# The last projection of layer 1 in PSUM banks of its own, and the final normalisation spread over VectorE, ScalarE and GpSimd

## The chip, the cores and the metric

One core of one Trainium2 chip runs the kernel. The metric is the device time of one execution in microseconds. A core has TensorE (matrix products, abbreviated PE in the profile, PEld for its weight loads), VectorE (DVE), ScalarE (ACT), GpSimd (POOL) and SyncE (SP), each with an instruction queue of its own; they wait for each other by semaphores. SBUF is the on-chip memory of 128 partitions, PSUM holds what TensorE puts out, in eight banks of 512 floats per partition.

## The reference, cut to what matters

A sequence of 2048 tokens with 256 features goes through two layers. Each has cross attention to 1601 context rows (16 heads), added through a gate, and a mixture of experts, added through another gate. Layer 1, which the change touches, is:

```python
out = jnp.einsum('bhnm,bmhd->bnhd', attn, v).reshape(B, N, IMAGE_DIM)
h = jax.nn.relu(out @ W1 + b1)              # 256 -> 512
return h @ W2 + b2                          # 512 -> 256: the attention's result
...
logits = jnp.einsum('bsd,de->bse', x, Wg) + bg
topk_vals, topk_idx = jax.lax.top_k(logits, TOP_K)      # 2 of 8 experts
topk_w = jax.nn.softmax(topk_vals, axis=-1)
h = jax.nn.relu(jnp.einsum('bsd,edf->bsef', x, W1) + b1)
eo = jnp.einsum('bsef,efd->bsed', h, W2) + b2
sel = jnp.take_along_axis(eo, topk_idx[..., None], axis=2)
mixed = jnp.sum(sel * topk_w[..., None], axis=2)
y = mixed + x
mu = jnp.mean(y, axis=-1, keepdims=True)
var = jnp.mean(jnp.square(y - mu), axis=-1, keepdims=True)
return gamma * (y - mu) * jax.lax.rsqrt(var + LN_EPS) + beta
...
x = x + jnp.tanh(g_ffn[1]) * _L1_ffn_ref(_layernorm(x, axis=-1), ...)
```

## The kernel before

The 2048 tokens lie as 16 tiles of 128 tokens, a token to a partition; four tiles make a block (four blocks). `x` is the running state, `xn` (a part of `xt`) its normalised copy. The program is a sequence of stages (`nc.Block()`), each ended by a barrier of all engines; within one, each engine's work is written out in order by hand, with semaphores between them. Nothing reorders it.

In the attention stage of a layer, TensorE makes scores and weighted sums for block after block. The projection of block b - 1 is woven into the scores of block b by `tail`: for layer 1 four calls of `hidden` (the 512 hidden features in four pieces of 128, each a product into PSUM bank 7, which VectorE reads through the relu into `hidT`) and then `output` for two pairs of tiles, also into bank 7, which VectorE reads into `y_tmp` and adds to `x`. Each piece waits for `s_read7`, that is until VectorE has read the one before. For the last block there are no more scores to weave into, so `for w in range(NC + 1): tail(NB, w)` runs the pieces one after the other. VectorE's part is `tail(NB, NB - 1)` at lines 1213 to 1240: after the updates it normalises the block (`norm_rows`), then come the transposes, the router's logits, the counts and slots of the routing, and GpSimd's 32 scatters of the tokens into the experts' lists.

The expert stage works through 39 tiles of 128 rows. For tile i, SyncE loads the rows, TensorE turns them (line 1542), VectorE copies them (1622), TensorE makes the first product (1555), VectorE adds the bias (1652), ScalarE takes the relu (1610), TensorE makes the second product (1567), VectorE adds its bias (1674), and GpSimd scatters the rows to `y_tok` with an indirect DMA (1738), which waits until the previous scatter has landed. In VectorE's order, `place` (lines 1634 and 1637: two instructions on one column that compute the row to which the result goes) stands between `hidden` and `finish`.

After the last scatter SyncE reads the results back, per block two reads of 512 KB (line 1515) into `got[0]` and `got[1]`, the second and first choice of each token. VectorE alone then does, for each block: `xn` plus weight times `got[0]` (1715), plus weight times `got[1]` (1720), statistics of the rows (421, 424), the reciprocal root by three Newton steps on four columns (426 to 436), the subtraction and scaling (439), times gamma (1727), plus beta (1728, gate folded into both by lines 1702 and 1703), and the addition to `x` (1729); SyncE writes the block out (1527).

## Time and profile before

| quantity | value |
|---|---|
| median of three runs | 1559.49 us (1559.07 to 1561.18) |
| profiled execution, its own time | 1561.43 us |
| its span, first to last instruction | 1559.7 us |
| TensorE busy | 1329.1 us (85%) |
| ScalarE busy | 958.1 us (61%) |
| VectorE busy | 576.2 us (37%) |
| GpSimd busy | 149.4 us (10%) |
| mean granted TensorE clock | 0.926 of full speed |

The profile is of one execution. Busy times add up what an engine's instructions took; a share averages over stages with different limits, so a change is read from the stage in which it lies. Times in the rows below are microseconds from the span's start.

### The profile page before, as it was taken

What the parts mean: (1) busy time and instruction counts of PE and PEld (TensorE: products, weight loads), DVE (VectorE), ACT (ScalarE), POOL (GpSimd) and SP (SyncE); (2) the same over time, 40 slices, a digit from 0 to 9 for tenths busy, and PEclk for the clock granted to TensorE, in tenths of its full rate; (3) what the DMA queues carried; (4) which work ended last, traced back from release to release, by engine and by line L of the source; (5) the groups of instructions that cost most, each with busy time, mean ns of one, the idle gap of its engine ahead of it and who ended that gap; (6) DMA issues with size and microseconds to landing.
All of it is one profiled execution on the core that took longest, in us unless ns stands there. A gap on an engine that the chain in (4) does not pass through costs nothing. (4 is left out here: it accounts for less than half of the span.)

```text
span 1559.7 us, 31895 instructions
## 1 busy us (share of the span) xinstructions
PE 1329.1 (85%) x13108; PEld 695.6 (45%) x13108; DVE 576.2 (37%) x1403; ACT 958.1 (61%) x1114; POOL 149.4 (10%) x157
## 2 busy tenths in 40 slices
PE   6899999999999988997479999999999750599920
PEld 4433333333335548996233343333343230499920
DVE  7412242331523433444522224224233232244458
ACT  3599999999993332332279969959969600244400
POOL 2000000000002341222000000000000005222210
PEclk9899999999999998999689999999999875799965
DMA  7680101010107141114186100100111132122241
GB/s 211 154 192 20 25 19 26 19 26 19 33 21 252 38 158 58 49 49 108 58 201 167 26 15 19 27 14 19 27 44 49 55 122 78 62 76 69 74 140 40
DMA packets 88875, 111.48 MB, mean 71 GB/s; under 512 B 10746, under 2 KB 75006, under 8 KB 87960
## 3 DMA queue, kind: packets, MB, share of 16 engines
q1 hardware_dynamic: 83448, 94.93, 22.5%
q0 software_dynamic: 5280, 14.47, 2.5%
q8 instruction: 107, 1.75, 0.5%
q14 instruction: 40, 0.33, 0.1%
HBM read 68.06 MB, written 36.81 MB: 67 GB/s over the span
## 5 line engine op out<-in xcount | busy, mean ns | idle before, releaser
L1119 ACT ACTIVATE arena<-ps 128x1024 f32<-128x1024 f32 x556 | 557.0, 1241 | 57.3 <-PE ps L917 57.3
L917 PE MATMUL ps<-arena 99*32 99x512 bf16 x6656 | 464.4, 384 | 13.6 <-PEq L767 9.6
L917 PEld LDWEIGHTS ps<-arena 99*32 99x32 bf16 x6656 | 150.1, 95 | 405.9 <-issue 166.9
L1119 ACT ACTIVATE wqkv<-ps 128x1024 f32<-128x1024 f32 x276 | 297.4, 1243 | 22.7 <-PE ps L917 22.7
L933 PE MATMUL ps<-arena 128*32 128x512 f32 x2224 | 289.3, 594 | 0.8 <-ACT arena L1119 0.8
L1201 DVE COPY work<-ps 128x512 f32<-128x512 f32 x32 | 22.1, 692 | 402.6 <-PE ps L933 402.6
L1555 PEld LDWEIGHTS ps<-work,arena 128*128 128x128 f32 x1184 | 144.6, 195 | 6.5 <-DVE work L1622 3.5
L1555 PE MATMUL ps<-work,arena 128*128 128x128 f32 x1184 | 145.7, 279 | 2.1 <-DVE work L1622 2.1
L933 PE MATMUL ps<-wqkv,arena 128*32 128x512 f32 x1104 | 143.2, 593 | 0.0
L1567 PE MATMUL ps<-arena,work 128*128 x496 | 117.2, 380 | 0.0
L1205 DVE RECIPROCAL work<-work 128x512 f32<-128x512 f32 x32 | 107.3, 3353 | 1.1
L1593 ACT ACTIVATE arena<-arena 128x1024 f32 x62 | 65.3, 1057 | 65.5 <-PEq L897 56.8
L1480 POOL DMA_INDIRECT list_x<-xt,slot x48 | 46.3, 964 | 579.4 <-DVE slot L1341 565.2
L933 PEld LDWEIGHTS ps<-arena 128*32 128x32 f32 x2224 | 68.2, 111 | 59.3 <-ACT arena L1119 2.7
L1567 PEld LDWEIGHTS ps<-arena,work 128*128 128x128 f32 x496 | 89.4, 190 | 10.1 <-issue 0.5
L1738 POOL DMA_INDIRECT y_tok<-work,dest x62 | 62.6, 1010 | 256.0 <-DVE work L1672 130.0
L1542 PE MATMUL ps<-ident,work 128*128 128x128 f32 x124 | 24.5, 281 | 62.5 <-DMA work<-list_x 62.5
L1622 DVE COPY work<-ps 128x256 f32<-128x256 f32 x62 | 26.3, 425 | 137.3 <-PE ps L1542 137.3
L1610 ACT ACTIVATE work<-work 128x512 f32<-128x512 f32 x39 | 24.6, 631 | 82.2 <-DVE work L1652 82.2
L1604 ACT ACTIVATE work<-ps 128x512 f32<-128x512 f32 x23 | 13.7, 597 | 89.3 <-PE ps L1555 89.3
L1468 POOL TENSOR_TENSOR arena<-arena 128x512 f32<-128x512 f32 x12 | 17.5, 1458 | 490.3 <-ACT arena L1139 490.3
L1226 DVE TENSOR_TENSOR work<-ps,b 128x512 f32<-128x512 f32 x16 | 11.1, 692 | 111.6 <-PE ps L958 111.6
(185 smaller groups left out, 1125.3 us busy)
## 6 DMA issues: line engine op xcount, KB each, us to landing
arena<-in_ew SPq DMA_DIRECT2D x16, 512.0 KB, 5.3
work<-list_x SPq DMA_DIRECT2D x62, 129.0 KB, 2.1
arena<-q_img SPq DMA_DIRECT2D x32, 192.0 KB
arena<-y_tok SPq DMA_DIRECT2D x12, 512.0 KB, 7.4
list_x<-zero SPq DMA_DIRECT2D x1, 5160.0 KB, 36.2
arena<-k_img SPq DMA_DIRECT2D x8, 624.0 KB, 12.4
q_img<-work SPq DMA_DIRECT2D x18, 256.0 KB, 2.5
k_img<-work SPq DMA_DIRECT2D x21, 208.0 KB, 2.4
```

The source lines that it names most:

```text
L917: last = nc.tensor.matmul(ps[i * VW:(i + 1) * VW, buf + j, :], k2[0:ROWS + SHIFT, h, at:at + VW], q2[0:ROWS + SHIFT, h, :], start=True, st ...
L933: last = nc.tensor.matmul(ps[j * VW:(j + 1) * VW, 6 + g % 2, :], v_aug[:, c, HG * g + j, :], probs[(b * STEPS + 2 * w + j // 2) % RING][:, ...
L1119: nc.scalar.activation(probs[(b * STEPS + u) % RING], ps[:, buf:buf + 2, :], ACT.Exp, scale=SCALE).then_inc(s_exp, 1)
L1205: nc.vector.reciprocal(sums, sums).then_inc(s_inv, 1)
L1480: nc.gpsimd.indirect_dma_start(out=list_x[l], out_offset=bass.IndirectOffsetOnAxis(ap=slot[:, i:i + 1], axis=0), in_=xt[:, i % NT, :], in_ ...
L1542: last = nc.tensor.transpose(ps[:, i % 2, k * P:(k + 1) * P], rows_in[i % 2][:, k * P:(k + 1) * P], ident[:, :])
L1555: last = nc.tensor.matmul(ps[:, 2 + 2 * (i % 2) + n, f * P:(f + 1) * P], w_now[i % 2][n][:, k, f * P:(f + 1) * P], rowsT[i % 2][:, k, :], ...
L1567: last = nc.tensor.matmul(ps[:, 6 + i % 2, 0:D], hT[i % 2][:, k, :], w_down[:, bass.ds(e, 1), k, :].rearrange("p a n -> p (a n)"), start=( ...
L1593: nc.scalar.activation(w_now[i % 2][0].rearrange("p k n -> p (k n)"), w_gate[l][:, bass.ds(e, 1), :, :].rearrange("p a k n -> p (a k n)"), ...
L1610: nc.scalar.activation(hT[i % 2], act_g[i % 2], ACT.Relu).then_inc(s_h, 1)
L1622: nc.vector.tensor_copy(rowsT[i % 2], ps[:, i % 2, 0:D].rearrange("p (k n) -> p k n", n=P)).then_inc(s_tc, 1)
L1738: nc.gpsimd.indirect_dma_start(out=y_tok[l], out_offset=bass.IndirectOffsetOnAxis(ap=dest[:, i % 4:i % 4 + 1], axis=0), in_=rows_out[i % 2 ...
```

## The change

It has three parts. First, the last block's projection of layer 1 is no longer made by `tail` but by a new `last_projection`: the four hidden pieces go to PSUM banks 0 to 3 without a wait between them, and the four output tiles to banks 4 to 7, with the loop over the hidden pieces outside, each waiting for its piece's relu. VectorE reads these banks (`own`).

Second, in the expert stage of layer 1, the scaling of gamma and beta by the gate goes to the start of VectorE's queue, and GpSimd adds beta to `x`, block by block, ahead of its first scatter.

Third, the final normalisation: ScalarE multiplies `got[0]` by its weight, GpSimd adds `xn`, VectorE adds `got[1]` times its weight and makes the statistics. The root is made once for eight tiles (`norm_root`, twice instead of four times), and gives a scale and a shift per row (`norm_scales`). ScalarE applies them tile by tile, GpSimd multiplies by gamma for two tiles at a time, and VectorE adds the product to `x` for two tiles at a time, all of it after the scales of both halves. SyncE's reads and writes stay.

```diff
@@ -100,6 +100,7 @@
         xt = sb("xt", [P, NT, DX])
         xn = xt[:, :, 0:D]
         zero = sb("zero", [P, DX])
+        scales = sb("scales", [P, 2, NT])
         dest_f = sb("dest_f", [P, 4])
         dest = sb("dest", [P, 4], U32)
         ctxT = sb("ctxT", [CH + 1, 2, MP])
@@ -414,12 +415,8 @@
             nc.gpsimd.iota(iota_tile[:, :], pattern=[[P, 48]], base=0, channel_multiplier=0,
                            allow_small_or_imprecise_dtypes=True)
-        def norm_rows(step, src, dst, n=TB):
-            for t in range(n):
-                last = nc.vector.bn_stats(stats[:, t, :], src(t))
-            step(last)
+        def norm_root(step, n):
             for t in range(n):
                 last = nc.vector.bn_aggr(mv[:, t, :], stats[:, t, :])
             step(last)
@@ -435,10 +432,29 @@
                 step(nc.vector.tensor_tensor(newton[:, 0:n], newton[:, 0:n], var_h[:, 0:n], ALU.mult))
                 step(nc.vector.scalar_tensor_tensor(out=rstd[:, 0:n], in0=newton[:, 0:n], scalar=1.5,
                                                     in1=rstd[:, 0:n], op0=ALU.add, op1=ALU.mult))
+        def norm_rows(step, src, dst, n=TB):
+            for t in range(n):
+                last = nc.vector.bn_stats(stats[:, t, :], src(t))
+            step(last)
+            norm_root(step, n)
             for t in range(n):
                 last = nc.vector.tensor_scalar(dst(t), src(t), mv[:, t, 0:1], rstd[:, t:t + 1], ALU.subtract,
                                                ALU.mult)
             return last
+        def norm_scales(step, src, n, scale, shift):
+            for t in range(n):
+                last = nc.vector.bn_stats(stats[:, t, :], src(t))
+            step(last)
+            norm_root(step, n)
+            nc.vector.tensor_copy(scale, rstd[:, 0:n])
+            return nc.vector.scalar_tensor_tensor(out=shift, in0=mv[:, 0:n, 0], scalar=-1.0, in1=rstd[:, 0:n],
+                                                  op0=ALU.mult, op1=ALU.mult)
         def layer(L):
             l = L.n
@@ -1064,9 +1080,28 @@
                         pe.wait_ge(s_ks, KD * (n + 1))
                         norm_sums(ps[:, 3, n * 4 * H:(n + 1) * 4 * H], squares1[n % 2], KC).then_inc(s_kn, 1)
+                    def last_projection():
+                        for i in range(2):
+                            pe.wait_ge(s_oc[i], NB * 16 * HG * NG // 2)
+                        pe.wait_ge(s_u, NB * NG)
+                        for f in range(4):
+                            for k in range(KD):
+                                last = nc.tensor.matmul(ps[:, f, :], w1[:, k, f * P:(f + 1) * P], oT[:, k, :],
+                                                        start=(k == 0), stop=(k == KD - 1))
+                            last.then_inc(s_full7, 1)
+                        for f in range(4):
+                            pe.wait_ge(s_read7, use(NB, f))
+                            for t in range(TB):
+                                last = nc.tensor.matmul(ps[:, 4 + t, 0:D],
+                                                        hidT[:, f, t * P:(t + 1) * P], w2[:, f, :],
+                                                        start=(f == 0), stop=(f == 3))
+                                if f == 3 and t % 2 == 1:
+                                    last.then_inc(s_full7, 1)
                     if l == 1:
-                        for w in range(NC + 1):
-                            tail(NB, w)
+                        last_projection()
                         last_turn()
                         last_logits()
                         counts()
@@ -1215,15 +1250,17 @@
                         group(now, NG - 1)
                         k = 0
+                        own = L.mlp and b == NB
                         if L.mlp:
                             for f in range(4):
                                 dve.wait_ge(s_full7, use(b, k))
-                                nc.vector.tensor_scalar(hidT[:, f, :], ps[:, 7, :], b1[:, f:f + 1], 0.0,
+                                nc.vector.tensor_scalar(hidT[:, f, :], ps[:, f if own else 7, :], b1[:, f:f + 1], 0.0,
                                                         ALU.add, ALU.max).then_inc(s_read7, 1)
                                 k += 1
                         for pair in range(2):
                             dve.wait_ge(s_full7, use(b, k))
                             nc.vector.tensor_tensor(y_tmp.rearrange("p (t d) -> p t d", d=D),
+                                                    ps[:, 4 + 2 * pair:6 + 2 * pair, 0:D] if own else
                                                     ps[:, 7, :].rearrange("p (t d) -> p t d", d=D), b2[:, :, :],
                                                     ALU.add).then_inc(s_read7, 1)
                             dve.wait_ge(s_read7, use(b, k))
@@ -1490,6 +1527,9 @@
+            s_gb, s_xb = sem(f"norm_params_scaled{l}"), sem(f"x_with_beta{l}")
+            s_w0, s_w1, s_sc = sem(f"first_weighed{l}"), sem(f"first_added{l}"), sem(f"norm_scales{l}")
+            s_nr, s_gm = sem(f"rows_normed{l}"), sem(f"rows_scaled_gamma{l}")
@@ -1614,6 +1654,18 @@
                         for c in range(NC):
                             act.wait_ge(s_v, c + 1)
                             copy_v(c, c % 4).then_inc(s_va, 1)
+                    else:
+                        for b in range(NB):
+                            act.wait_ge(s_back[b], 16 * L.top)
+                            for t in range(b * TB, (b + 1) * TB):
+                                last = nc.scalar.activation(got[0][:, t, :], got[0][:, t, :], ACT.Identity,
+                                                            scale=wts[:, 2, t:t + 1])
+                            last.then_inc(s_w0, 1)
+                        for t in range(NT):
+                            act.wait_ge(s_sc, t // (2 * TB) + 1)
+                            nc.scalar.activation(got[0][:, t, :], got[0][:, t, :], ACT.Identity,
+                                                 bias=scales[:, 1, t:t + 1], scale=scales[:, 0, t:t + 1]
+                                                 ).then_inc(s_nr, 1)
                 @block.vector
                 def _(dve):
@@ -1675,6 +1727,11 @@
                                                     eb2[:, bass.ds(e, 1), :].rearrange("p a n -> p (a n)"), ALU.add
                                                     ).then_inc(s_y, 1)
+                    tg = tgate[:, 2 + l:3 + l]
+                    chain = Chain(dve, f"back_chain{l}")
+                    if l == 1:
+                        nc.vector.tensor_scalar(gamma, gamma, tg, None, ALU.mult)
+                        nc.vector.tensor_scalar(beta, beta, tg, None, ALU.mult).then_inc(s_gb, 1)
                     copy_rows(0)
                     if l == 0:
                         copy_up(0)
@@ -1696,40 +1753,43 @@
                             copy_up(i + 2)
                     finish(NTL - 1)
-                    tg = tgate[:, 2 + l:3 + l]
-                    chain = Chain(dve, f"back_chain{l}")
-                    if l == 1:
-                        nc.vector.tensor_scalar(gamma, gamma, tg, None, ALU.mult)
-                        chain(nc.vector.tensor_scalar(beta, beta, tg, None, ALU.mult))
-                    for b in range(NB):
-                        ts = slice(b * TB, (b + 1) * TB)
-                        dve.wait_ge(s_back[b], 16 * L.top)
-                        if l == 0:
+                    if l == 0:
+                        for b in range(NB):
+                            ts = slice(b * TB, (b + 1) * TB)
+                            dve.wait_ge(s_back[b], 16)
                             chain(nc.vector.scalar_tensor_tensor(
                                 out=x[:, ts, :].rearrange("p t d -> p (t d)"),
                                 in0=got[0][:, ts, :].rearrange("p t d -> p (t d)"), scalar=tg,
                                 in1=x[:, ts, :].rearrange("p t d -> p (t d)"), op0=ALU.mult, op1=ALU.add))
                             chain(norm_rows(chain, lambda t: x[:, b * TB + t, :], lambda t: xn[:, b * TB + t, :]))
-                            continue
-                        for t in range(b * TB, (b + 1) * TB):
-                            last = nc.vector.scalar_tensor_tensor(out=xn[:, t, :], in0=got[0][:, t, :],
-                                                                  scalar=wts[:, 2, t:t + 1], in1=xn[:, t, :],
-                                                                  op0=ALU.mult, op1=ALU.add)
-                        chain(last)
-                        for t in range(b * TB, (b + 1) * TB):
-                            last = nc.vector.scalar_tensor_tensor(out=got[0][:, t, :], in0=got[1][:, t, :],
-                                                                  scalar=wts[:, 1, t:t + 1], in1=xn[:, t, :],
-                                                                  op0=ALU.mult, op1=ALU.add)
-                        chain(last)
-                        chain(norm_rows(chain, lambda t: got[0][:, b * TB + t, :], lambda t: got[0][:, b * TB + t, :]))
-                        gb = gamma.unsqueeze(1).broadcast_to([P, TB, D])
-                        bb = beta.unsqueeze(1).broadcast_to([P, TB, D])
-                        chain(nc.vector.tensor_tensor(got[0][:, ts, :], got[0][:, ts, :], gb, ALU.mult))
-                        chain(nc.vector.tensor_tensor(x[:, ts, :], x[:, ts, :], bb, ALU.add))
-                        nc.vector.tensor_tensor(x[:, ts, :], x[:, ts, :], got[0][:, ts, :], ALU.add).then_inc(s_xf, 1)
+                    else:
+                        n = 2 * TB
+                        for i in range(2):
+                            for b in range(2 * i, 2 * i + 2):
+                                dve.wait_ge(s_w1, b + 1)
+                                for t in range(b * TB, (b + 1) * TB):
+                                    last = nc.vector.scalar_tensor_tensor(out=got[0][:, t, :], in0=got[1][:, t, :],
+                                                                          scalar=wts[:, 1, t:t + 1],
+                                                                          in1=got[0][:, t, :], op0=ALU.mult,
+                                                                          op1=ALU.add)
+                            chain(last)
+                            norm_scales(chain, lambda t: got[0][:, i * n + t, :], n, scales[:, 0, i * n:(i + 1) * n],
+                                        scales[:, 1, i * n:(i + 1) * n]).then_inc(s_sc, 1)
+                        for t in range(0, NT, 2):
+                            dve.wait_ge(s_gm, t // 2 + 1)
+                            last = nc.vector.tensor_tensor(x[:, t:t + 2, :], x[:, t:t + 2, :], got[0][:, t:t + 2, :],
+                                                           ALU.add)
+                            if t % TB == TB - 2:
+                                last.then_inc(s_xf, 1)
                 @block.gpsimd
                 def _(pool):
+                    if l == 1:
+                        pool.wait_ge(s_gb, 1)
+                        for b in range(NB):
+                            nc.gpsimd.tensor_tensor(x[:, b * TB:(b + 1) * TB, :], x[:, b * TB:(b + 1) * TB, :],
+                                                    beta.unsqueeze(1).broadcast_to([P, TB, D]), ALU.add
+                                                    ).then_inc(s_xb, 1)
                     for i in range(NTL):
                         pool.wait_ge(s_de, i + 1)
                         pool.wait_ge(s_y, i + 1)
@@ -1741,6 +1801,17 @@
                     if l == 0:
                         ones_row(pool, 2)
                         pad_v(Chain(pool, "v_pad_chain1"))
+                    else:
+                        for b in range(NB):
+                            ts = slice(b * TB, (b + 1) * TB)
+                            pool.wait_ge(s_w0, b + 1)
+                            nc.gpsimd.tensor_tensor(got[0][:, ts, :], got[0][:, ts, :], xn[:, ts, :], ALU.add
+                                                    ).then_inc(s_w1, 1)
+                        for t in range(0, NT, 2):
+                            pool.wait_ge(s_nr, t + 2)
+                            nc.gpsimd.tensor_tensor(got[0][:, t:t + 2, :], got[0][:, t:t + 2, :],
+                                                    gamma.unsqueeze(1).broadcast_to([P, 2, D]), ALU.mult
+                                                    ).then_inc(s_gm, 1)
         for L in layers:
```

## Rows read from the trace of the kernel before

**Rows 1.** Chain of work that ended last: start us, duration us, what.
```profile
1495.93 2.41 DMA y_tok<-work,dest
...
1498.83 4.99 DMA arena<-y_tok
...
1508.77 0.39 DVE mv L424 x4
...
1511.44 0.17 DVE root_bits L436
...
1553.94 1.23 DVE x L1729
```

**Rows 2.** Timeline, GpSimd: start us, us, engine, line, operation, [idle before <- released by].
```profile
1354.75 0.96 POOL L1738 DMA_INDIRECT y_tok<-work,dest  x1 [19.05 <-DVE work L1674]
```

**Rows 3.** Timeline, last projection of layer 1.
```profile
1244.35 3.75 PE L945 MATMUL ps<-work,w 128*128 128x512 f32 x4 [9.49 <-issue]
...
1253.57 1.98 PE L945 MATMUL ps<-work,w 128*128 128x512 f32 x4 [0.85 <-DVE work L1221]
...
1259.32 3.69 PE L958 MATMUL ps<-w,work 128*128 128x256 f32 x16 [0.94 <-DVE work L1221]
...
1269.20 1.41 DVE L421 BATCH_NORM_STATS2 stats<-x 128x6 f32<-128x256 f32 x4
```

**Rows 4.** Stretches: us; busy PE, PEld, DVE, ACT, POOL; PE clock; DMA.
```profile
1252.00:1253.00 1.00, 0.73 (x1) 0.00 (x0) 0.23 (x1) 0.00 (x0) 0.00 (x0) 0.67 1.10 364
...
1348.00:1349.00 1.00, 0.48 (x3) 0.14 (x2) 0.42 (x1) 0.00 (x0) 0.00 (x0) 0.88 0.00 0
```

**Rows 5.** Timeline, start of layer 1's expert stage.
```profile
1340.81 3.98 SPq L1504 DMA_DIRECT2D work<-list_x  x3
...
1349.77 0.20 DVE L1634 TENSOR_SCALAR dest_f<-work,tilef 128x1 f32<-128x1 f32 x1
```

**Rows 6.** Timeline, two GpSimd additions in layer 0's shared expert.
```profile
497.23 0.72 POOL L1473 TENSOR_TENSOR x<-x,arena 128x256 f32<-128x256 f32 x1 [0.84 <-ACT arena L1148]
...
499.93 1.27 POOL L1468 TENSOR_TENSOR arena<-arena 128x512 f32<-128x512 f32 x1 [0.25 <-ACT arena L1139]
```

**Rows 7.** Timeline, GpSimd and VectorE beside each other.
```profile
525.23 4.29 DVE L1306 TENSOR_SCALAR xt<-xt,wts 128x256 f32<-128x256 f32 x16
...
527.18 3.46 POOL L1468 TENSOR_TENSOR arena<-arena 128x512 f32<-128x512 f32 x1 [2.68 <-ACT arena L1139]
...
535.44 0.29 DVE L1337 TENSOR_TENSOR work<-work,padc 128x128 f32<-128x128 f32 x1
535.60 1.27 POOL L1468 TENSOR_TENSOR arena<-arena 128x512 f32<-128x512 f32 x1 [3.62 <-ACT arena L1139]
535.76 1.25 DVE L1339 TENSOR_TENSOR work<-work,oh 128x128 f32<-128x128 f32 x1
```

**Rows 8.** Groups by shape: busy us, mean ns | idle before (L1211: 1234 to 1275.5).
```profile
L1715 DVE SCALAR_TENSOR_TENSOR xt<-arena,wts,xt 128x256 f32<-128x256 f32 x16 | 6.7, 478 | 10.1 <-DMA arena<-y_tok 10.1
L421 DVE BATCH_NORM_STATS2 stats<-arena 128x6 f32<-128x256 f32 x16 | 5.6, 414 | 0.1
...
L1211 DVE TENSOR_TENSOR work<-work 128x512 f32<-128x512 f32 x1 | 0.7, 693 | 0.1
...
L1593 ACT ACTIVATE arena<-arena 128x1024 f32 x62 | 65.3, 1057 | 65.5 <-PEq L897 56.8 <-issue 6.6
L1610 ACT ACTIVATE work<-work 128x512 f32<-128x512 f32 x39 | 24.6, 631 | 82.2 <-DVE work L1652 82.2
```

**Rows 9.** Reads of expert rows: timeline row, then the issue's KB and us to landing.
```profile
1499.92 0.51 SPq L1515 DMA_DIRECT2D arena<-y_tok  x1
arena<-y_tok SPq DMA_DIRECT2D x1, 512.0 KB, 8.2
...
1504.88 1.83 SPq L1515 DMA_DIRECT2D arena<-y_tok  x1
arena<-y_tok SPq DMA_DIRECT2D x1, 512.0 KB, 9.1
```

## The prediction, made before the changed kernel was run

> **What bounds the kernel now.** I read the chain of work that ended last first, from its end backwards. It ends in VectorE: from the landing of the first expert rows at 1503.8 us to the last addition at 1555.2 us nothing but VectorE works [rows 1]. Before that lies one read of 5 us, and before that a chain of scatters: the first of layer 1's 39 starts at 1354.75 us, released by the first tile's result [rows 2], the last at 1495.93 us, to land at 1498.34 [rows 1]. So one scatter and its wait take (1498.34 - 1354.75)/39 = 3.68 us. In the waits of that stretch nearly every scatter is released by the landing of the one before; the chain view hands over to TensorE at 1405 us, where it names the scatter's destination column, but that column is for a tile still to come. TensorE needs about as much per tile, so I take the whole stretch as a stiff piece: it starts when the first scatter starts and its length stays. The third place is the last projection of layer 1's attention, between 1244.35 and 1269.20 us [rows 3]: there TensorE and VectorE take turns on one PSUM bank, and all that follows (routing, lists, experts) waits. The change touches these three places and nothing else on the path.
>
> **Part 1, last projection in its own banks.** Before, one hidden piece is made, VectorE reads it, the next one is made. After, the sixteen TensorE instructions of the four hidden pieces are issued without a wait, and then the 32 of the output, ordered by piece, so that they need piece 3 only for their last eight. At the high clock four 512-column instructions took 1.98 us and sixteen 256-column ones 3.69 [rows 3]: with p for 512 columns and e for the pipeline's end, 4p + e = 1.98 and 8p + e = 3.69, so p = 0.43 and e = 0.27. At the low clock p is 0.86 (there four took 3.75). What decides is when the granted clock goes from 1.2 to 2.4 GHz. Before, it did in the slice 1252 to 1253 (mean 0.67, so at 1252.7), 8.3 us after TensorE's start at 1244.35 with one pause of 0.8 us. At the start of layer 1's experts it rose at 1348.25 (mean 0.88 of the slice 1348 to 1349) [rows 4], 4 to 5.5 us after the first dense work. With a rise at 1252.7, ten hidden instructions run low and six high: 8.6 + 2.6 = 11.2 us, to 1255.5; with a rise at 1248.5, five low and eleven high: 4.3 + 4.7 = 9.0, to 1253.3. The output adds 32 x 0.215 + 0.25 = 7.1 us: end at 1262.6 or 1260.4. VectorE's four relus (one pass over 512 columns each, about 0.7 us [rows 8]) hide under the later hidden pieces and the first 24 output instructions. At the end, though, both pairs are ready nearly together: the first 0.86 us before the second, and each needs an addition and an update, about 1.5 us together. So statistics start about 2.2 us after TensorE's end, where before they started one such pair of passes, 1.5 us, after it: 1264.8 or 1262.6 instead of 1269.2, a gain of 4.4 to 6.6 us. I take 5.5, between the two observed rises, since TensorE is now busier than in the first case. The pause until the transposes stays about 8 us, so the low clock there stays too.
>
> **Part 2, start of layer 1's expert stage.** The two scalings of gamma and beta go ahead of VectorE's first tile. The stage's first transfer is issued at 1340.81 [rows 5]; VectorE then waits for rows that TensorE can only turn after that transfer has landed, so they cost nothing. New on GpSimd's queue, ahead of all 39 scatters, are four additions of beta on 128x1024. GpSimd's 128x512 addition takes 1.27 us and its 128x256 one 0.72 [rows 6], so 1024 columns by the same slope take 1.27 + 2 x 0.55 = 2.37 us: 9.5 us for four, from about 1341.8 (the transfer's issue, and two scalings of 0.4) to 1351.3. The first scatter came at 1354.75, so about 3 us of cover are left. The other path is the shared access of the two engines to SBUF. When VectorE worked from 525.23 to 529.52, a GpSimd addition begun at 527.18 took 3.46 us instead of 1.27, that is until VectorE's stream ended; the other way, VectorE's 128x128 product with both inputs in SBUF took 1.25 us beside a GpSimd addition, against 0.29 for the same shape alone [rows 7]. Each waits out the other. In the expert loop the two small instructions of each tile that compute the destination (lines 1634, 1637) have all operands in SBUF, and they stand between the rows' copy and the result's copy in VectorE's order. The first tile's pair stands in VectorE's long wait for TensorE's second tile, where two waits of at most 2.37 us nearly fit. The second tile's pair, at 1349.8 [rows 5], meets the last addition: it ends at about 1352.0 instead of 1350.2, of which VectorE's later slack leaves about 0.5 us for the first result. Bounds: 0, and 2.5 us (one whole addition). I take 0.5, all of which shifts the scatters.
>
> **Part 3, the final normalisation.** I lay it out in the old time scale, with GpSimd and VectorE excluding each other wherever VectorE has all operands in SBUF. Prices: VectorE's weighted sum of 256 columns 6.7/16 = 0.42, its statistics 5.6/16 = 0.35 (one input, not excluded), an addition of 512 columns 0.69 [rows 8], four aggregations 0.39 and the root after them, to 1511.61, 2.4 us whatever the number of rows [rows 1]; GpSimd 2.37 and 1.27 as above; ScalarE 0.63 us for 512 and 1.06 for 1024 columns [rows 8], so 0.42 for 256, some 0.33 of it in a stream. Block 0 is in at 1503.8 [rows 1], block 1 at 1499.92 + 8.2 = 1508.1, block 3 at 1504.88 + 9.1 = 1514.0 [rows 9], block 2 between, about 1511.
> - ScalarE weighs block 0 to 1505.3, GpSimd adds to 1507.7. Block 1: ScalarE 1509.5, GpSimd 1511.9. VectorE's sums of block 0 lie between; those of block 1 run 1511.9 to 1513.6 and hold GpSimd's third addition back to 1513.6 to 1516.0; the fourth ends 1518.4.
> - VectorE: eight statistics and eight aggregations to 1517.3, the root held until 1518.4, then 2.4 + 0.35 us: first scales at 1521.2.
> - VectorE's eight sums of blocks 2 and 3 to 1524.6, which hold GpSimd's gamma products; these run 1524.6 to 1529.9 (four, 1.27 each). Statistics to 1528.2, the root mostly behind those products: second scales at 1532.5.
> - VectorE's four first additions to 1535.2; then four products and four additions in turns, 4 x (1.27 + 0.69) = 7.9 us, to 1543.1.
> The end was 1555.2, so the part gains 12 us. GpSimd gets 4 x 2.37 + 8 x 1.27 = 19.6 us of work, and VectorE keeps 16 x 0.42 + 5.6 + 1.6 + 2 x 2.75 + 8 x 0.69 = 24.9. The last transfer is as large as before, and its 4.5 us to the end stay.
>
> The rows show this exclusion for a stream of TENSOR_SCALARs and for one TENSOR_TENSOR [rows 7], not for a wide SCALAR_TENSOR_TENSOR. If the latter did not hold GpSimd, the third addition would end at 1514.9, the first four products at 1526.5, and the last addition at about 1541, a gain of 14. The Trainium skill, page "SBUF — State Buffer", section "Who interferes with whom", says that any VectorE instruction with two SBUF inputs contends with a GpSimd instruction that reads SBUF and that the later one blocks fully; by it the gain is 12. No row here tests that shape.
>
> **Sum.** On the profiled execution: 1561.43 - 5.5 + 0.5 - 12.0 = 1544.4 us. Its span is 1559.7, with 1.7 outside; the median of the runs, 1559.49, lies 1.9 below it, so the same sum on the median is 1542.5.
>
> **Rivals.**
> - A, the exclusion is weaker than laid out (long additions do not hold each other). Then the same schedule without holds gives first scales at 1520.1, second at 1529.9, the last addition at 1536.4: gain 18.8, in all 5.5 + 18.8 - 0.2, that is 1535.4. Against it stand both pairs of [rows 7]; for it, that they show few shapes.
> - B, exclusion worse: every stretch of GpSimd and VectorE in the tail is serial. 24.9 (VectorE) + 19.6 (GpSimd) + 2.1 (ScalarE) = 46.6 us from 1503.8: end at 1550.4, gain 4.8. With 4.4 from the projection and 2.5 lost at the start: 1559.5 - 6.7 = 1552.8. Against it: statistics and transfers do overlap.
> - C, slower than before: GpSimd's price for 128x1024 is not on the line through 256 and 512. Place: the four additions ahead of the scatters, then the tail. With a factor s on all GpSimd work the start costs 9.5s - 13.0 + 0.5 (13.0 from 1341.8 to the first scatter), the tail 19.6(s - 1) - 12; with -5.5 the sum is zero at s = 1.7, that is 4.0 us for 128x1024; at s = 2 it is +8.6, 1568.1. The two measured sizes lie on a plain line with a small constant, so I give it little.
> - D, the projection brings nothing, since the clock stays low through it (16 x 0.86 + 32 x 0.43 + 0.5 = 28.0 us of TensorE, and 1.5 for VectorE: statistics at 1273.9, 4.7 later than before): -12 + 0.5 + 4.7, 1552.7. Against it, the rise came in both examples within 8.3 us.
>
> **How the numbers follow.** Forecast 0.65, A 0.17, B 0.10, C 0.04, D 0.04. The range leaves out most of B, C and D: low 1535.0, from A; high 1549.0, from the forecast with its bad ends (-4.4 + 2.5 - 9, where 9 is midway between the 12 laid out and the 5 of B, a bit above). Under 0.2%, 3 us, this kernel's change can't be told from none. Faster by more is all but C and the worst of B and D: 0.95; same 0.02; slower 0.03.
>
> **What would show it.** Part 1: one stretch of TensorE without pauses from the first hidden piece to the last output, statistics 18.3 to 20.5 us after its start, against 24.9. Part 2: first scatter 13.9 to 16.5 us after the stage's first transfer, against 13.9; GpSimd's additions at 2.4 us, lines 1634 and 1637 stretched to about 2 us for one or two tiles. Part 3: GpSimd's products stretched beside VectorE's weighted sums, the small root instructions stretched beside products, and some 39 us from block 0's landing to the last addition, against 51.4. The prediction is wrong if GpSimd's 128x1024 takes over 3 us, if the scatter chain gets longer in itself, or if additions and products run side by side.

## The result, and the profile after

The changed kernel takes 1543.19 us (median of four, three of them 1541.6 to 1544.5) beside 1559.28 for the kernel before (1557.18 to 1561.18): a ratio of 0.9893, 95% interval 0.9876 to 0.9910, or 16.7 us less. Forecast were 1542.5 us and a range of 1535.0 to 1549.0.

Three executions took much longer than the others of their kernel (3394.7 us here, and beside the experiments 3008.46 of the kernel before and 1701.61 of e2) and enter no ratio, and as the profile that came with these runs is of the first of them, in which TensorE's products took over twice their usual time (the bf16 ones 0.79 us each for 0.38), "after" below (e1) is a further execution of the same kernel, beside which the kernel before was run on the same chip.

> The changed kernel once more, to read its stages at the usual TensorE clock. Theory (sum of parts -5.5, +0.5, -12): about 1542.5 us; projection stretch from TensorE's first hidden instruction to the statistics 18.3 to 20.5 us; first scatter about 14.4 us after the expert stage's first transfer; block 0's landing to last addition 41 us. Rival (the whole gain comes from the tail, the projection gains nothing because of the clock): the first stretch stays at 24 to 29 us and the tail is under 35 us.

Measured: 1549.74 us (1547.28 to 1551.87) on a chip where the kernel before takes 1566.34; ratio 0.9894 [0.9876, 0.9912]. Its page, span and two of the engines:

```profile
span 1547.6 us, 31882 instructions
PE 1326.8 (86%) x13108; PEld 695.4 (45%) x13108; DVE 563.7 (36%) x1345; ACT 973.0 (63%) x1146; POOL 179.8 (12%) x173
```

GpSimd has 30 us more of work, ScalarE 15, VectorE 13 less, though VectorE's busy time holds waits for GpSimd, as will be seen. The span fell by 12.1 us only, because the changed part began 5.2 us later (TensorE's first hidden piece at 1249.56, before at 1244.35 [rows 3]). Nothing is changed ahead of it, and from profile to profile that start lies anywhere between 1240.9 and 1252.1. So single spans are not compared here but stretches of the path, from row to row, in us:

| kernel | P | R | E | T | start of P |
|---|---|---|---|---|---|
| before | 24.85 | 71.6 | 157.6 | 61.3 | 1244.35 |
| after (e1) | 18.28 | 71.2 | 157.5 | 51.05 | 1249.56 |
| after (e12) | 19.10 | 71.1 | 158.2 | 50.6 | |
| e2, projection alone | 18.28 | 71.2 | 157.1 | 61.1 | 1247.32 |
| e3, all but the projection | 24.84 | 71.1 | 158.1 | 50.3 | 1252.12 |
| e4, beta's additions alone | 23.05 | 71.4 | 159.4 | 55.9 | 1248.62 |
| e5, busy before P | 16.21 | 71.1 | 157.7 | 50.3 | 1240.88 |
| e6, half of the products | 18.46 | 71.0 | 157.3 | 46.5 | |
| e7, additions twice | 17.90 | 71.1 | 158.4 | 50.5 | |
| e8, one root | 18.03 | 71.0 | 157.1 | 46.2 | |
| e9, busy to the lists | 16.21 | 71.6 | 157.3 | 49.7 | |
| e10, busy to the experts | 16.21 | 70.3 | 158.9 | 49.9 | |
| e11, e10 and e8 | 16.22 | 68.7 | 156.8 | 45.3 | |

P runs from the first hidden piece of the last projection to the statistics, R from there to the first load of layer 1's expert stage, E from that load to the issue of the reads of the results, T from that issue to the end of the span. One profile stands behind each row, and the same code does not repeat exactly: P lies between 17.9 and 19.1 with the new projection (16.2 with extra products ahead of it) and between 23.05 and 24.85 with the old one, R between 71.0 and 71.6 and E between 157.1 and 159.4 (e10 and e11, with extra products in both, left aside), T between 49.7 and 51.05 with the tail of e1. A difference between two rows that is smaller than that shows nothing by itself.

Part 1. The timeline of the last projection, which answers to [rows 3], and the slice in which the clock rose, which answers to [rows 4]:

```profile
1249.56 9.17 PE L1091 MATMUL ps<-work,w 128*128 128x512 f32 x16 [9.50 <-DMA work<-work]
1258.57 7.07 PE L1097 MATMUL ps<-w,work 128*128 128x256 f32 x32
...
1267.84 1.41 DVE L440 BATCH_NORM_STATS2 stats<-x 128x6 f32<-128x256 f32 x4
```

```profile
1253.00:1254.00 1.00, 1.00 (x3) 0.49 (x2) 0.65 (x1) 0.00 (x0) 0.00 (x0) 0.64 0.94 289
```

TensorE has no pause between its 16 hidden instructions and its 32 of the output. The mean clock of 0.64 in the slice puts the rise at 1253.7, 4.2 us after the start; before it came 8.3 us after it.

Part 2. The start of the expert stage, which answers to [rows 2] and [rows 5]:

```profile
1339.02 16.21 SPq L1544 DMA_DIRECT2D work<-list_x  x6
1340.13 9.28 POOL L1790 TENSOR_TENSOR x<-x,wqkv 128x1024 f32<-128x1024 f32 x4 [5.79 <-DVE wqkv L1734]
1342.74 2.06 DVE L1689 TENSOR_TENSOR dest<-dest_f,work 128x1 uint32<-128x1 f32 x1
...
1348.11 1.33 DVE L1689 TENSOR_TENSOR dest<-dest_f,work 128x1 uint32<-128x1 f32 x1
...
1352.84 0.98 POOL L1798 DMA_INDIRECT y_tok<-work,dest  x1 [3.43 <-DVE work L1726]
1356.64 0.96 POOL L1798 DMA_INDIRECT y_tok<-work,dest  x1 [2.82 <-DVE work L1726]
```

GpSimd's four additions take 2.32 us each, and VectorE's first two small instructions on the destination each wait for the one that is running (2.06 and 1.33 us, the next takes 0.16). But GpSimd is free at 1349.41, and the first scatter comes 13.82 us after the first load, before 13.94 [rows 2, 5].

Part 3. The timeline of the tail, from the last scatter on. (On SyncE's rows, SPq, the time is the queue's.)

```profile
1494.07 0.96 POOL L1798 DMA_INDIRECT y_tok<-work,dest  x1 [2.21 <-DMA y_tok<-work,dest]
1496.55 8.80 SPq L1555 DMA_DIRECT2D arena<-y_tok  x8
...
1501.76 1.70 ACT L1661 ACTIVATE arena<-arena,wts 128x256 f32<-128x256 f32 x4 [13.17 <-DMA arena<-y_tok]
1503.54 2.16 POOL L1808 TENSOR_TENSOR arena<-arena,xt 128x1024 f32<-128x1024 f32 x1 [8.52 <-ACT arena L1661]
...
1510.76 3.65 DVE L1771 SCALAR_TENSOR_TENSOR arena<-arena,wts 128x256 f32<-128x256 f32 x4 [3.34 <-POOL arena L1808]
...
1514.44 2.71 DVE L452 BATCH_NORM_STATS2 stats<-arena 128x6 f32<-128x256 f32 x8
...
1520.51 7.27 DVE L1771 SCALAR_TENSOR_TENSOR arena<-arena,wts 128x256 f32<-128x256 f32 x8
1520.63 4.04 ACT L1666 ACTIVATE arena<-arena,scales 128x256 f32<-128x256 f32 x8 [6.29 <-DVE scales L456]
1521.80 5.71 POOL L1812 TENSOR_TENSOR arena<-arena,wqkv 128x512 f32<-128x512 f32 x4 [5.21 <-ACT arena L1666]
...
1533.90 9.17 DVE L1780 TENSOR_TENSOR x<-x,arena 128x512 f32<-128x512 f32 x8
...
1535.19 6.73 POOL L1812 TENSOR_TENSOR arena<-arena,wqkv 128x512 f32<-128x512 f32 x4 [7.68 <-ACT arena L1666]
```

From block 0's landing (1501.72) to the end of the last addition (1543.07) are 41.35 us, where before it was 51.4 [rows 1]. The row to look at is VectorE's eight weighted sums at 1520.51: they take 7.27 us, 0.91 each, where the same instruction took 0.42 before [rows 8]. One by one, the sums and GpSimd's products in that stretch are:

```profile
1522.10 1.49 DVE L1771 SCALAR_TENSOR_TENSOR arena<-arena,wts 128x256 f32<-128x256 f32 x1
1523.26 1.44 POOL L1812 TENSOR_TENSOR arena<-arena,wqkv 128x512 f32<-128x512 f32 x1
1523.51 1.48 DVE L1771 SCALAR_TENSOR_TENSOR arena<-arena,wts 128x256 f32<-128x256 f32 x1
1524.67 1.44 POOL L1812 TENSOR_TENSOR arena<-arena,wqkv 128x512 f32<-128x512 f32 x1
1524.91 1.48 DVE L1771 SCALAR_TENSOR_TENSOR arena<-arena,wts 128x256 f32<-128x256 f32 x1
```

They alternate, one sum to one product. A sum takes 1.48 us, of which 0.4 is its own and the rest a product waited out; a product takes 1.44, its own 1.27 [rows 6] and hardly more. It is VectorE that is held.

### The profile page after: what moved, and what is told of

Same layout as the page of the kernel before. It is cut to its first block and busy times, and to the rows that moved or that the text cites. A ratio compares the mean times of both kernels' runs of the same rounds, so it can differ in the third digit from the quotient of the medians.

```text
span 3392.9 us, 31882 instructions
## 1 busy us (share of the span) xinstructions
PE 3217.4 (95%) x13108; PEld 1369.7 (40%) x13108; DVE 555.7 (16%) x1345; ACT 1049.7 (31%) x1146; POOL 177.6 (5%) x173
## 5 line engine op out<-in xcount | busy, mean ns | idle before, releaser
L933 PE MATMUL ps<-arena 99*32 99x512 bf16 x6656 | 1037.4, 791 | 9.6 <-PEq L783 9.6
L933 PEld LDWEIGHTS ps<-arena 99*32 99x32 bf16 x6656 | 316.6, 163 | 1022.1 <-issue 884.5
L949 PE MATMUL ps<-arena 128*32 128x512 f32 x2224 | 702.1, 1361 | 0.0
L949 PE MATMUL ps<-wqkv,arena 128*32 128x512 f32 x1104 | 348.8, 1364 | 0.0
L1595 PEld LDWEIGHTS ps<-work,arena 128*128 128x128 f32 x1184 | 324.2, 386 | 25.3 <-issue 20.6
L1595 PE MATMUL ps<-work,arena 128*128 128x128 f32 x1184 | 326.3, 488 | 2.1 <-DVE work L1674 2.1
L1607 PE MATMUL ps<-arena,work 128*128 x496 | 269.1, 737 | 0.0
L1607 PEld LDWEIGHTS ps<-arena,work 128*128 128x128 f32 x496 | 158.1, 328 | 74.1 <-issue 68.3
L949 PEld LDWEIGHTS ps<-wqkv,arena 128*32 128x32 f32 x1104 | 60.4, 185 | 99.4 <-issue 97.7
L974 PE MATMUL ps<-w,work 128*128 128x256 f32 x160 | 92.3, 763 | 0.0
```

The source lines that it names most:

```text
L933: last = nc.tensor.matmul(ps[i * VW:(i + 1) * VW, buf + j, :], k2[0:ROWS + SHIFT, h, at:at + VW], q2[0:ROWS + SHIFT, h, :], start=True, st ...
L949: last = nc.tensor.matmul(ps[j * VW:(j + 1) * VW, 6 + g % 2, :], v_aug[:, c, HG * g + j, :], probs[(b * STEPS + 2 * w + j // 2) % RING][:, ...
L974: last = nc.tensor.matmul(ps[:, 7, half * D:(half + 1) * D], src[:, k, t * P:(t + 1) * P], w2[:, k, :], start=(k == 0), stop=(k == ks - 1) ...
L1595: last = nc.tensor.matmul(ps[:, 2 + 2 * (i % 2) + n, f * P:(f + 1) * P], w_now[i % 2][n][:, k, f * P:(f + 1) * P], rowsT[i % 2][:, k, :], ...
L1607: last = nc.tensor.matmul(ps[:, 6 + i % 2, 0:D], hT[i % 2][:, k, :], w_down[:, bass.ds(e, 1), k, :].rearrange("p a n -> p (a n)"), start=( ...
```

## The experiments

### The three parts alone

The first two leave out one part or the other, the third has one step alone. e2 has the projection alone:

```diff
                     if l == 1:
-                        for w in range(NC + 1):
-                            tail(NB, w)
+                        last_projection()
...
```

> The kernel before with the last projection in its own banks alone. Theory: 5.5 us faster than before (4.4 to 6.6), since the pauses go and the clock still rises within 8.3 us of the start. Rival (clock stays low): 4 to 5 us slower than before.

Measured: 1558.63 us, ratio 0.9951 [0.9934, 0.9967], 7.7 us less. P is 18.28, 6.57 less, with the rise of the clock as early as in e1; R, E and T stand as before. The part by itself is real: 6.6 us by P, 5.2 to 10.3 by the interval. Not all of P's gain is the banks', as e4 will show.

e3 is the changed kernel with the old projection (parts 2 and 3, for the tail needs beta in x):

```diff
                     if l == 1:
-                        last_projection()
+                        for w in range(NC + 1):
+                            tail(NB, w)
...
```

> The changed kernel with the last projection as before (one bank, in turns). Theory: 11.5 us faster than the kernel before, being -12 for the final normalisation and +0.5 for beta's additions ahead of the scatters. Rival (no exclusion between GpSimd and VectorE): 18.6 faster. Together with the projection alone it should give the whole change; if the two sum to more than 2 us off the whole, the parts act on each other.

Measured: 1554.22 us, ratio 0.9920 [0.9902, 0.9938], 12.5 us less. P is back at 24.84, T is 11.0 shorter. By the ratios the two gains add up to 20.2 us, where the whole gained 16.6. That is 3.6 off, more than the 2 us named beforehand as a sign that the parts act on each other, but each of the three ratios is uncertain by about 2.7 us either way, so it decides nothing. By the stages P's 6.57 in e2 and T's 11.0 in e3 make 17.6, and in e1 the same two stages gained 6.57 and 10.24, 16.8: within the spread of T, so no sign that the parts act on each other.

e4 has part 2 alone, VectorE's tail being as before without its additions of beta (line 1728):

```diff
+                    if l == 1:
+                        pool.wait_ge(s_gb, 1)
+                        for b in range(NB):
+                            nc.gpsimd.tensor_tensor(x[:, b * TB:(b + 1) * TB, :], x[:, b * TB:(b + 1) * TB, :],
+                                                    beta.unsqueeze(1).broadcast_to([P, TB, D]), ALU.add
+                                                    ).then_inc(s_xb, 1)
...
-                        chain(nc.vector.tensor_tensor(x[:, ts, :], x[:, ts, :], bb, ALU.add))
+                        dve.wait_ge(s_xb, b + 1)
```

> The kernel before, in which GpSimd adds beta to x ahead of its scatters and VectorE no longer does so at the end; the rest of the final normalisation as before. Theory: four VectorE additions of 1.25 us go from the path and the scatters start 0.5 us later: 4.5 us faster than before. Rival (beta's additions delay the first scatter by a whole addition, 2.5 us, or more through exclusion in the first tiles): 2.5 us faster or less. If the additions were hidden completely: 5.0 faster.

Measured: 1561.26 us, ratio 0.9973 [0.9962, 0.9985], 4.2 us less. T is 5.4 shorter: four additions of 1.22 us off VectorE, with their steps between. E is 1.8 longer in its profile. The additions need not be the cause: e1 has them too and an E of 157.5; here both of the first two tiles' products ran at the low clock.

```profile
1346.71 3.78 PE L1556 MATMUL ps<-work,arena 128*128 128x128 f32 x16 [0.52 <-DVE work L1623]
...
1351.43 3.79 PE L1556 MATMUL ps<-work,arena 128*128 128x128 f32 x16 [0.52 <-DVE work L1623]
```

At the high clock these sixteen take 1.95 to 2.05 us; before and in e1 the second tile's already did. This profile gives something unasked for as well. It has the old projection, yet P is 23.05 instead of 24.85, since its clock rose 4.3 us after the start, as early as in e1:

```profile
1248.62 3.75 PE L945 MATMUL ps<-work,w 128*128 128x512 f32 x4 [9.49 <-issue]
...
1253.22 1.98 PE L945 MATMUL ps<-work,w 128*128 128x512 f32 x4 [0.85 <-DVE work L1221]
```

Here the second piece is already fast, in [rows 3] only the third. So of the 6.57 us between e1 and before, 4.8 are the banks (23.05 - 18.28), and 1.8 the earlier rise (24.85 - 23.05), which the old order can have too. Only e4's profile has the old order with an early rise, so the split stands on one profile.

### What the clock is worth in the projection: e5

Ten products into a free bank, with nothing to wait for, ahead of the projection (each shows as two instructions in the rows):

```diff
                     def last_projection():
+                        for _ in range(10):
+                            nc.tensor.matmul(ps[:, 0, :], ident[:, :], w1[:, 0, :], start=True, stop=True)
```

> The changed kernel with ten extra products on TensorE, into a bank that nothing reads, in its 9.5 us wait ahead of the last projection (8.6 us at 2.4 GHz), to keep the clock up. Theory (the size of part 1 hangs on when the clock rises; in the changed kernel's profile it rose 4.1 us after the start, after five hidden instructions at 0.86 us): all 16 run at 0.43 us, the stretch from first hidden product to the statistics falls from 18.3 to 16.1 us, and TensorE's extra work moves nothing else. Rival (TensorE's rate there is set by something other than the clock, such as weight loads or the DMA traffic of the experts' weights): it stays at 18.3.

```profile
1231.30 8.85 PE L1087 MATMUL ps<-w,ident 128*128 128x512 f32 x20
...
1240.88 7.11 PE L1093 MATMUL ps<-work,w 128*128 128x512 f32 x16 [0.73 <-issue]
...
1257.09 1.40 DVE L440 BATCH_NORM_STATS2 stats<-x 128x6 f32<-128x256 f32 x4
```

The sixteen hidden instructions take 7.11 us, 0.44 each, instead of 9.17, and P is 16.21. The whole: 1541.65 us beside 1560.41, ratio 0.9882 [0.9866, 0.9899]. By P, a clock that is high from the start is worth 2.1 us over e1 and up to 2.9 over e12; the ratio can't tell it from e1's.

### Whether the start of the scatters sets their end: e7

Each of GpSimd's four additions done twice, with half of beta each time, so that GpSimd has 18.6 us ahead of the first scatter:

```diff
-                        nc.vector.tensor_scalar(beta, beta, tg, None, ALU.mult).then_inc(s_gb, 1)
+                        nc.vector.tensor_scalar(beta, beta, tg, 0.5, ALU.mult, ALU.mult).then_inc(s_gb, 1)
...
-                        for b in range(NB):
+                        for i in range(2 * NB):
+                            b = i % NB
+                            if i >= NB:
+                                pool.wait_ge(s_xb, i - NB + 1)
```

> Beta is added in two halves, so eight additions of 128x1024 stand on GpSimd's queue ahead of the first scatter instead of four. Theory (chain of scatters is stiff, cover 3 us): GpSimd is free at about 19.7 us after the stage's first transfer, the first scatter comes at 19.8 instead of 13.8 us after it, the chain from there stays at 143.7 us, and the whole is 6 us slower than the changed kernel. Rival (the chain has slack, since TensorE sets its pace and a scatter alone takes 3.2 us of TensorE's 3.73): it catches up, the whole is under 2 us slower.

```profile
1332.95 18.55 POOL L1793 TENSOR_TENSOR x<-x,wqkv 128x1024 f32<-128x1024 f32 x8 [5.68 <-DVE wqkv L1734]
1351.64 0.99 POOL L1801 DMA_INDIRECT y_tok<-work,dest  x1
1354.87 0.96 POOL L1801 DMA_INDIRECT y_tok<-work,dest  x1 [2.24 <-DVE dest L1689]
...
1355.99 2.05 PE L1595 MATMUL ps<-work,arena 128*128 128x128 f32 x16 [1.18 <-DVE work L1674]
...
1358.04 0.96 POOL L1801 DMA_INDIRECT y_tok<-work,dest  x1 [2.22 <-DVE dest L1689]
...
1477.67 0.96 POOL L1801 DMA_INDIRECT y_tok<-work,dest  x1 [2.78 <-DVE work L1726]
1481.40 0.96 POOL L1801 DMA_INDIRECT y_tok<-work,dest  x1 [2.77 <-DVE work L1726]
```

The first scatter comes 19.80 us after the first load, 6.0 later than in e1, but E is only 0.8 longer, and the whole (1543.41 us, ratio 0.9893 [0.9873, 0.9913]) is e1's. The scatters start at a spacing of 3.2 us while they are behind, and later at 3.73, released by VectorE's result of the tile. In e1 the first five stand 3.73 to 3.80 apart, and up to the last few tiles the chain of work that ended last goes through TensorE's products, one tile per 3.73 us. The scatters follow TensorE; they are not a chain whose start fixes its end. The late start did reach TensorE once: from the fifth tile on a destination column is written only when the scatter four tiles back has landed, and VectorE's wait for the first scatter's landing (to 1354.10) made TensorE pause 1.18 us. That can be the 0.8; it can also be the spread of E.

### Who holds whom in the tail: e6 and e8

In e6 GpSimd doesn't make the first four products (the first eight tiles are left without gamma), and VectorE's first four additions wait for ScalarE instead (not shown); nothing else is changed:

```diff
-                        for t in range(0, NT, 2):
+                        for t in range(NT // 2, NT, 2):
                             pool.wait_ge(s_nr, t + 2)
```

> Leaves out the multiplication by gamma for the first eight tiles (GpSimd's four products); all else as in the changed kernel. Theory (GpSimd and VectorE exclude each other, and VectorE's eight weighted sums beside those products take 7.27 us instead of 3.3): the sums take 3.3 us and the end comes 3.9 us sooner. Rival (the sums are slow for another reason): they stay at 7.3 us and the end comes at the same time.

```profile
1515.22 3.25 DVE L1771 SCALAR_TENSOR_TENSOR arena<-arena,wts 128x256 f32<-128x256 f32 x8
1518.51 2.71 DVE L452 BATCH_NORM_STATS2 stats<-arena 128x6 f32<-128x256 f32 x8
```

With no products of GpSimd beside them the eight sums take 3.25 us instead of 7.27, and T is 46.5, some 4 less. The whole: 1539.94 us, ratio 0.9867 [0.9851, 0.9884]. The four products cost VectorE 4.0 us, all on the path.

e8 leaves GpSimd only its four additions of `xn`, gathers the statistics of all sixteen tiles under one root, and makes the products on VectorE:

```diff
+                        chain(last)
+                        norm_root(chain, NT)
...
+                        for h in range(4):
+                            for t in range(h * TB, (h + 1) * TB, 2):
+                                dve.wait_ge(s_nr, t + 2)
+                                nc.vector.tensor_tensor(got[0][:, t:t + 2, :], got[0][:, t:t + 2, :],
+                                                        gamma.unsqueeze(1).broadcast_to([P, 2, D]), ALU.mult
+                                                        ).then_inc(s_gm, 1)
```

> The changed kernel with the final normalisation regrouped: one root for 16 tiles, VectorE's sums of blocks 2 and 3 behind the statistics of 0 and 1, and the products by gamma on VectorE (0.6 us for two tiles against 1.27 on GpSimd, in the same excluded time). Theory (exclusion): scales 25.5 us after block 0's landing, then 16 x 0.6 us and 1.1 for ScalarE: last addition at 36.5 us instead of 41.3, 4.8 us faster. Rival (GpSimd's products run for free beside VectorE): VectorE's extra 4.8 us outweigh the root saved, no faster than the changed kernel.

```profile
1509.61 3.24 DVE L1769 SCALAR_TENSOR_TENSOR arena<-arena,wts 128x256 f32<-128x256 f32 x8
...
1519.70 7.98 ACT L1666 ACTIVATE arena<-arena,scales 128x256 f32<-128x256 f32 x16 [12.90 <-DVE scales L1780]
...
1529.63 1.29 DVE L1791 TENSOR_TENSOR x<-x,arena 128x512 f32<-128x512 f32 x2
```

From block 0's landing (1494.37) to the last addition (1530.92) are 36.5 us, against 41.35. VectorE makes a product and an addition in 0.6 us each, so that a pair costs 1.2, where GpSimd's product and VectorE's addition in turns cost 1.68 (6.73/4). The whole: 1537.73 us, ratio 0.9856 [0.9839, 0.9872]. The forecast of 4.8 us for this regrouping came in (36.5 for 36.5). e8 changes the number of roots, the order of VectorE's work and the engine of the products together, so it doesn't show what each is worth; together with e6 it shows that here GpSimd's products cost VectorE more than they took from it.

### Whether the clock can be kept high further on: e9, e10, e11

e9 adds to e5 eight products after the projection and three after the logits:

```diff
                         last_projection()
+                        for _ in range(8):
+                            nc.tensor.matmul(ps[:, 0, :], ident[:, :], w1[:, 0, :], start=True, stop=True)
                         last_turn()
                         last_logits()
+                        for _ in range(3):
+                            nc.tensor.matmul(ps[:, 0, :], ident[:, :], w1[:, 0, :], start=True, stop=True)
                         counts()
```

> The changed kernel with extra products on TensorE (results unused) ahead of the last projection (ten), between it and the transposes (eight, 6.9 us in an 8.5 us wait) and between the router's logits and the counts (three). Theory (the low clock after each pause is what these short stages pay): projection stretch 16.1 us instead of 18.3; transposes 1.0 instead of 2.0 us, logits about 1.7 instead of 3.1, counts 1.2 instead of 2.1; statistics to the last slot cast 22.6 us instead of 25.9; in all 5.5 us faster than the changed kernel. Rival (those short products are bound by weight loads or waits that do not follow the clock): the part behind the projection gains under 1 us, in all 2 to 3.

Two stretches, the transposes and the logits after them:

```profile
1265.00:1268.00 3.00, 1.09 (x8) 0.86 (x8) 1.44 (x5) 0.30 (x1) 0.00 (x0) 1.00 0.00 0
...
1268.00:1272.00 4.00, 3.16 (x15) 3.16 (x16) 0.00 (x0) 0.79 (x2) 0.00 (x0) 0.51 0.00 0
```

```profile
1272.27 5.47 PE L1112 MATMUL ps<-w,ident 128*128 128x512 f32 x6
1277.53 0.99 PE L1042 MATMUL ps<-oh,below 128*128 128x256 f32 x2
```

The transposes run at 1.00 and take 1.09 us instead of 1.97. Then, from about 1268, the clock is low again (0.51 in the logits' slice, TensorE busy 3.16 of 4 us; the eight dense products had ended at 1264.90), and the three products meant to keep it high take 5.47 us at the low clock and hold up the counts. 1540.77 us, ratio 0.9898 [0.9876, 0.9920]: nothing won over e12 beside it (1542.45, 0.9901) that can be told.

e10 adds to that ten products when all but eight of GpSimd's scatters into the lists are issued, and two ahead of the first tile of the experts:

```diff
                         counts()
+                        pe.wait_ge(s_mark, 1)
+                        for _ in range(10):
+                            nc.tensor.matmul(ps[:, 0, :], ident[:, :], w1[:, 0, :], start=True, stop=True)
...
+                    if l == 1:
+                        for _ in range(2):
+                            nc.tensor.matmul(ps[:, 2, :], ident[:, :], w1[:, 0, :], start=True, stop=True)
                     turn_rows(0)
```

> The same, and twelve extra products around the start of layer 1's expert stage. Theory: the first product of the first tile runs in 1.95 us instead of 3.78 and the second tile's never runs low, so first load to first scatter falls from 13.8 to about 11.7 us, unless GpSimd's four additions of beta (free at 10.4 us after the first load, scatter possible at 10.5) bind; from the first load to the read of the results 155.5 us instead of 157.5. In all 7.5 us faster than the changed kernel. Rival (the scatters' chain sets the end and not TensorE): the read of the results comes no sooner, in all 5.5.

```profile
1322.00:1328.00 6.00, 6.00 (x15) 2.47 (x13) 0.00 (x0) 0.00 (x0) 4.22 (x5) 1.00 0.25 89
...
1332.30:1336.00 3.70, 3.67 (x5) 1.53 (x6) 0.62 (x2) 2.00 (x2) 2.60 (x2) 0.50 0.27 74
```

```profile
1332.33 3.75 PE L1627 MATMUL ps<-w,ident 128*128 128x512 f32 x4 [4.10 <-PEq L915]
...
1337.03 3.78 PE L1608 MATMUL ps<-work,arena 128*128 128x128 f32 x16 [0.52 <-DVE work L1690]
```

The ten do bring the clock to 1.00, but the stage's barrier leaves a pause of 4.1 us behind them, after which it is at 0.50 again, and the first product of the experts takes 3.78 us as ever. 1541.31 us, ratio 0.9889 [0.9870, 0.9909], the same as e12.

e11 puts e8's tail and all of e10's products together:

> The version the experiments point to: the extra products of all three places and the final normalisation with one root and the products by gamma on VectorE. If the parts do not act on each other: 7.5 + 4.8 = 12.3 us faster than the changed kernel.

Measured: 1534.54 us beside 1557.34 for the kernel before and 1542.45 for the changed kernel (e12), ratio 0.9853 [0.9838, 0.9868]. That is 7.9 us faster than the changed kernel. By the stages of the two profiles it would be 12.0 (T 5.3, P 2.9, R 2.3, E 1.4); T and P alone make 8.2, and R's and E's part is not borne out by the runs. Expected were 12.3. In this profile the same extra products did bring the clock up in time: behind a pause of 3.65 us it rose at 1329.1, and the first product of the experts is fast:

```profile
1325.88 3.64 PE L1627 MATMUL ps<-w,ident 128*128 128x512 f32 x4 [3.65 <-PEq L915]
...
1330.26 2.05 PE L1608 MATMUL ps<-work,arena 128*128 128x128 f32 x16 [0.52 <-DVE work L1690]
```

So they work in one profile (e11) and not in the other (e10). e11 has the lowest median here, 1.5% under the kernel before, but e8 with the same tail and none of the extra products has the same ratio (0.9856 [0.9839, 0.9872]): no ratio shows that the extra products are worth anything.

e12 is the changed kernel itself beside these three:

> The changed kernel once more, on the same chip as the three before it, as their measure: 0.9893 of the kernel before, stretches as in its last profile (18.3 us for the projection if the clock rises after 4 us, up to 20.5 if after 8; 157.5 from first load to the read of the results; 41.3 from block 0's landing to the last addition).

Measured: 1542.45 us, ratio 0.9901 [0.9883, 0.9919].

## Why the prediction was right, and where it was not

The total was right (1542.5 for 1543.19), and each part's gain was close to its place; three steps under it were not.

**Part 1, forecast 5.5 us of 4.4 to 6.6, measured 6.6 (e1, e2) and 5.75 (e12).** Right, mechanism and size. The statistics came 18.28 us after the start, at the early end of the 18.3 to 20.5 forecast. The two prices taken from [rows 3] hold: 0.43 us for 512 columns gave 7.11 us for sixteen in e5, and 32 outputs took 7.07 for 7.1. The uncertain term was the clock's rise. From slices of 1 us as in [rows 4] it came 3.4 (e7), 3.7 (e8), 4.2 (e1, e2), 4.5 (e6) and 5.8 us (e12) after the start with the new order, and 4.3 (e4), 8.3 (before) and 8.4 (e3) with the old. e12, of the same kernel as e1, has its rise at 1250.0, from a start at 1244.17:

```profile
1249.00:1250.00 1.00, 1.00 (x2) 0.34 (x1) 0.00 (x0) 0.00 (x0) 0.00 (x0) 0.50 0.96 326
1250.00:1251.00 1.00, 1.00 (x4) 0.38 (x2) 0.23 (x1) 0.00 (x0) 0.00 (x0) 1.00 1.08 380
```

So the lower bound of the forecast (18.3) was a little too high (17.90 in e7, 18.03 in e8) and the upper one was not reached. The reason given for a value between the two observed rises, that TensorE is busier after the change, is not shown: e4 has an early rise with the old, broken order, and what sets the moment stays open. The rise moved by 2.4 us between profiles of the new order and by 4.1 between those of the old, so that the forecast of 5.5 lies this close to the measured 5.75 and 6.6 is in part luck. Rival D, a clock low through the projection, occurred in no profile.

**Part 2, forecast a loss of 0.5 us of 0 to 2.5, measured nothing.** GpSimd's addition was costed at 2.37 us and took 2.32; the small instructions were stretched to 2.06 and 1.33 us as forecast. The step that failed is "a stiff piece: it starts when the first scatter starts and its length stays". Doubling the additions moved the first scatter by 6.0 us and the end by 0.8. The average of 3.68 us per scatter was read as what a scatter needs; it is what TensorE needs (3.73), and a scatter that is behind follows after 3.2. The chain view's handing over to TensorE at 1405, set aside in the prediction, was the true reading. Had the cover been short, the loss would have been overcounted. Rival C (GpSimd's 128x1024 far dearer) is out at 2.16 to 2.32 us.

**Part 3, forecast 12.0 us, measured 10.2 in e1; the mean of T over the profiles with this tail (e1, e3, e5, e7, e9, e10, e12: 50.35) makes it 10.9.** The exclusion was the right mechanism, and the wide SCALAR_TENSOR_TENSOR, for which no row stood, has it: in e6 the sums go from 7.27 to 3.25 us when GpSimd's products are gone. Rival A (no holds, 18.8) is out. The Trainium skill, page "SBUF — State Buffer", section "Who interferes with whom", says that a VectorE instruction with two SBUF inputs contends with a GpSimd instruction that reads SBUF, and calls the lock exclusive. Here the trace agrees: 1.48 us for a sum of 0.4 beside a product of 1.27. Rival B (all in series, 46.6 us) is out at 41.35: in e1's rows VectorE's statistics (1514.44 to 1517.15) overlap GpSimd's fourth addition (1514.41 to 1516.59).

But the step "which hold GpSimd's gamma products; these run 1524.6 to 1529.9" had the roles the wrong way round. From [rows 7], where a stream of TENSOR_SCALARs kept GpSimd waiting to its end, it took it that VectorE's stream keeps the pair of engines to itself. The runs show turns, one instruction each, and then the engine with the short instructions loses: a sum of 0.4 us waits 1.1 for each product. The three steps of the sum, from block 0's landing:

| step | forecast | after (e1) |
|---|---|---|
| first scales ready | 17.4 | 18.9 |
| second scales ready | 28.7 | 32.3 |
| last addition ends | 39.3 | 41.35 |

The first term lost 1.5 us: ScalarE's four tiles took 1.70 us, where some 1.4 were taken, block 1 landed 5.0 us after block 0 instead of 4.3, and its four sums, meeting GpSimd's third addition, took 3.65 us (block 0's four, with nothing beside them, 1.67). It was not VectorE's stream that held that addition back. Against these some 2.9 us stand 1.1 that the forecast had set down for holding the root until the fourth addition ended, which did not happen, and 0.3 of shorter statistics. The second lost another 2.1: 3.9 for the sums' waits for products (7.27 for 3.4), less the 1.8 that the forecast had set down mostly for holding the root back, which never happened: GpSimd was done with the products before it. The third got 1.5 back: pairs of product and addition took 1.68 us (6.73/4) instead of 1.96, and GpSimd's products began 1.2 us after the scales, beside VectorE's four first additions, which the forecast had put ahead of them (2.75 us). That makes 2.05 us more on the path in all.

**The sum.** Forecast 17.0 us (5.5 - 0.5 + 12.0), by stages 17.3 in e1 (6.57 + 0.43 + 0.07 + 10.24), by ratio 16.6. The total is closer than its terms: part 1 came out 1.1 us better in e1 and part 2 0.5 better, part 3 1.8 worse, and that these cancel is luck.

## What to carry to other kernels

Before work is given to GpSimd beside VectorE, list VectorE's instructions with all operands in SBUF that run then: each can wait out one GpSimd instruction, so the loss is the number of such meetings times most of GpSimd's duration (here four meetings with products of 1.27 us cost 4.0), and short VectorE instructions lose most for what they do. This was seen for sums and additions with two inputs in SBUF; the one stream of TENSOR_SCALARs in these traces did not give way. A constant pitch of a chain of transfers is no evidence that the transfers set it: compare it with the pace of the engine that feeds them, or put a delay ahead of the chain and see whether its end moves. For a serial piece on one PSUM bank, separate banks are worth what the turns cost (here 4.8 us, by the one pair of profiles with the same early rise of the clock); the clock's share on top (up to 2.9 us of P) comes and goes from run to run.
